# One fused two-block kernel: the coordinate gates and the folding of the wavelet weights put into the first convolution's stage, and a new order of work in the wavelet stage

## The reference, cut to what is touched

```python
# coordinate gate: depends on weights and on positions only, never on x
hdn  = relu(einsum('oi,bihw->bohw', w1, coords) + b1)      # 2 -> 32 channels
gate = sigmoid(einsum('oi,bihw->bohw', w2, hdn) + b2)      # 32 -> 192 channels
# per level l = 0 (64x64) and l = 1 (32x32):
cx = wt_fwd(cur)                        # 2x2 Haar step, 4 bands per channel
t  = dwconv(cx, dw_w[l]); t = einsum('coi,bcihw->bcohw', mix_w[l], t) + mix_b[l]
t  = t * gate[l]
hlow = strip_pool(t, 3); ho = hl*hlow + (1+hh)*(t-hlow)    # 7-wide means
vlow = strip_pool(ho, 2); vo = vl*vlow + (1+vh)*(ho-vlow)
t  = t*beta + vo*gamma
t  = t * sigmoid(einsum('coi,bci->bco', sb_w[l], mean(t)) + sb_b[l]) * wscale[l]
# then both levels back up (iwt), times sigmoid(fuse_gate), plus the 5x5
# depthwise "base" convolution; channel mean/max and row sums for attention
```

## Time and profile before

| what | value |
|---|---|
| median of 3 runs | 2800.9 us (2799.82 to 2801.34) |
| the profiled execution's own time | 2798.28 us |
| its span, first to last instruction | 2796.5 us |
| granted TensorE clock, mean | 0.916 of full |
| PE busy | 2339.4 us (84%) |
| DVE busy | 1596.0 us (57%) |
| ACT busy | 1013.3 us (36%) |
| POOL busy | 536.7 us (19%) |

### The profile page before, as it was taken

How to read it: one execution, slowest core, us unless ns; L and a number is a source line. 1 busy time by engine, 2 the same in 40 slices (tenths; PEclk the granted TensorE clock), 3 DMA queues, 4 the chain that set the end, 5 groups by cost and what they waited for, 6 DMA issues and landing times. The chain is left out here.

```text
span 2796.5 us, 62141 instructions
## 1 busy us (share of the span) xinstructions
PE 2339.4 (84%) x21290; PEld 1273.4 (46%) x21290; DVE 1596.0 (57%) x2838; ACT 1013.3 (36%) x1923; POOL 536.7 (19%) x833
## 2 busy tenths in 40 slices
PE   5767749999969999997399999999994999688887
PEld 2333438777743333331156666666662232233332
DVE  3334411111127777775078888888882445477776
ACT  3344411111118888884100000000000112377776
POOL 7510000000000000003055555665550000000000
PEclk9888869999989999996579999999997899799999
DMA  6987888777737777774655555555543999433332
GB/s 140 249 224 208 212 250 276 267 266 261 270 91 137 147 147 147 147 143 99 133 117 129 123 129 132 130 129 121 130 107 87 229 250 267 120 102 107 103 104 79
DMA packets 550647, 454.97 MB, mean 163 GB/s; under 512 B 335272, under 2 KB 464480, under 8 KB 547136
## 3 DMA queue, kind: packets, MB, share of 16 engines
q1 hardware_dynamic: 417490, 418.23, 57.0%
q10 hardware_dynamic: 129024, 15.75, 4.8%
q0 software_dynamic: 4032, 19.53, 2.9%
HBM read 270.23 MB, written 183.74 MB: 162 GB/s over the span
## 5 line engine op out<-in xcount | busy, mean ns | idle before, releaser
L556 PE MATMUL gate_ps<-gate_data,gate_wt 64*64 64x289 f32 x6144 | 384.3, 408 | 53.2 <-DMA gate_data<-y 39.6
L556 PEld LDWEIGHTS gate_ps<-gate_data,gate_wt 64*64 64x64 f32 x6144 | 311.9, 133 | 125.6 <-issue 60.3
L875 ACT CAST mix_h<-mix_bank 96x512 f16<-96x512 f32 x512 | 267.6, 593 | 7.0 <-PE mix_bank L826 3.2
L596 DVE TENSOR_TENSOR gate_out<-gate_gelu,gate_ps 128x578 f32<-128x578 f32 x96 | 72.6, 757 | 345.0 <-PE gate_ps L556 339.4
L1137 POOL MEMSET cg_image<- 48x7680 f32 x1 | 6.5, 6491 | 1131.7 <-POOLq L58 1131.7
L286 DVE COPY exp_out<-exp_y 128x384 f32<-128x384 f32 x192 | 102.8, 567 | 154.6 <-PE exp_y L249 153.0
L573 ACT ACTIVATE gate_gelu<-gate_ps 128x578 f32<-128x578 f32 x96 | 62.7, 653 | 351.6 <-PE gate_ps L556 351.6
L2012 PE MATMUL fus_bank<-fus_xt,fus_taps 76*32 76x512 f32 x1344 | 159.5, 626 | 27.2 <-DMA fus_shift<-gate_shift 24.3
L957 DVE TENSOR_SCALAR mix_hb<-mix_h,mix_b1q 96x1024 f16<-96x1024 f16 x256 | 122.7, 479 | 93.6 <-ACT mix_h L875 93.6
L826 PE MATMUL mix_bank<-mix_xq,mix_w1q 112*96 112x512 fp8e5 x512 | 143.5, 382 | 29.1 <-ACT mix_h L875 23.0
L965 DVE CAST mix_hq<-mix_hb 96x2048 fp8e5<-96x2048 f16 x128 | 156.5, 1223 | 19.8 <-DVE mix_hb L957 17.9
(11 more groups left out here) (220 smaller groups left out, 4316.8 us busy)
## 6 DMA issues: line engine op xcount, KB each, us to landing
y<-exp_out SPq DMA_DIRECT2D x64, 816.0 KB, 12.3
gate_data<-y SPq DMA_DIRECT2D x24, 2176.0 KB, 15.2
g<-gate_out SPq DMA_DIRECT2D x48, 578.0 KB, 3.6
mix_sc<-g SPq DMA_DIRECT2D x31, 816.0 KB
gate_wt<-wm SPq DMA_DIRECT2D x96, 256.0 KB, 4.8
wav_strips<-xp SPq DMA_DIRECT2D x96, 204.0 KB, 2.9
wav_halves<-xp SPq DMA_DIRECT2D x48, 340.0 KB, 4.4
wav_conv<-wav_lines ACTq DMA_DIRECT2D x384, 40.0 KB
```

What stands on the lines that cost most here:

```text
L556: mm = pe.matmul(banks(a, v)[64 * g:64 * (g + 1), r], wt[q][64 * r:64 * (r + 1), 2 * a + g, n, :], src, start=n == 0, stop=n == 3)
L875: act.copy(h16[at.pair][:, m, h, :], bank[(2 * m + h) % len(bank)][0:HID, :]).then_inc(h16_ready, 1)
```

## The change

Four things change.

1. The stage `coordinate_gates` is gone. Its gate maps are made at the head of `gated_conv`: ACT and GpSimd load the small inputs, PE does ten 2-row and twenty 32-row matmuls before its first convolution matmul, ACT does 3 relus and 10 sigmoids of 1024 columns, and SP stores 20 blocks in runs of 4 KB. SP no longer waits for `cleared` before its first loads, and `data_in` is split by v.
2. The weight folding runs on GpSimd inside `gated_conv` (`wavelet_weights`), behind the gates' stores and the first items. DVE's coefficient tables now stand at the head of the wavelet stage, behind its memsets.
3. In the wavelet's laps PE does `up` for done, after `band_conv_0`, in place of `up` for tail at the end; `low_band` waits for `ct_ready` of two channels back. DVE takes `gate_0` before `add_base`, splits `box_0` around `sums`, and takes `weigh` before `gate_1`.
4. ACT takes over the reflected columns of `init`, the scaled matrices, `logit_w` and `base_w` (from DVE and GpSimd); four of the eight `conv1` loads go to SP; `conv0` and `low_w` become one tile, `front_w`, with one load per half.

```diff
 def gated_conv
             @block.sync
-                sp.wait_ge(cleared, 1)
                 load_weights(0, 0)
                 load_data(0, 0)
+                sp.wait_ge(data_in[0][0], 16)
...
             @block.tensor
+                pe.wait_ge(coords_in, 16 * 10)
+                for n, groups in enumerate((4, 4, 2)):
+                    for g in range(groups):
+                        x = pe.matmul(hidden_banks[n][HD * g:HD * (g + 1), :], cg_w1[HD * g:HD * g + 2, n // 2, :],
+                                      xy[HD * g:HD * g + 2, n, :], start=True, stop=True)
+                pe.wait_ge(maps_in, 16 * 9)
+                pe.wait_ge(relued, 3)
+                for j, (lvl, m, g) in enumerate(JOBS):        # 10 jobs
+                    if j > 1:
+                        pe.wait_ge(gate_ready, j - 1)
+                    for r in range(2):
+                        x = pe.matmul(ps[1][j % 2][0:HID, NT * r:NT * (r + 1)],
+                                      cg_w2[HD * g1:HD * (g1 + 1), lvl, HID * m:HID * (m + 1)],
+                                      hid[2 if lvl else r][HD * g1:HD * (g1 + 1), :], start=True, stop=True)
+                pe.wait_ge(gate_ready, len(JOBS))
...
+            @block.gpsimd
+                pool.wait_ge(gates_out, 16 * 2 * len(JOBS))
+                pool.wait_ge(out_ready, 2 + 8)
+                wavelet_weights(nc, pool, t, tab, k, stage)
 def wavelet
             @block.tensor
                 def low_band(i, u):
+                    if second(i):
+                        pe.wait_ge(ct_ready, 2 * i + u - 1)
                 def step(front, tail, done):
                         band_conv_0(*front)
+                    if done is not None:
+                        up(*done)
                     if tail is not None:
                         mix(*tail)
...
                         base_conv(*front)
-                    if tail is not None:
-                        up(*tail)
             @block.scalar
+                    for lvl, box, scaled in ((0, box0, scaled0), (1, box1, scaled1)):
+                        for m in range(2):
+                            x = act.activation(scaled[u][:, m, :], box[:, :], ACT.Copy, scale=table(coefs[lvl], n)[:, 2 + m:3 + m])
...
             @block.vector
                 def step(front, tail, done):
+                        gate_0(*front)
                         add_base(*done)
-                        gate_0(*front)
-                        box_0(*front)
+                        box_0(*front, 0)
                         sums(*tail)
-                        gate_1(*front)
+                        box_0(*front, 1)
                         weigh(*tail)
+                        gate_1(*front)
                         collect(*done)
```

More of the change, by code:

```diff
@@ L514, in _ @@
                 load_data(0, 1)
+                for j, (lvl, m, g) in enumerate(JOBS):
+                    sp.wait_ge(gate_ready, j + 1)
+                    for o2 in range(2):
+                        if lvl == 0:
+                            at = S1 * g + P8 * (2 * m + o2)
+                            to = t["gate0"][:, at:at + P8].rearrange("c i r x -> c (i r x)")
+                        else:
+                            at = S1 * (2 * m + o2)
+                            to = t["gate1"][:, at:at + S1].rearrange("c i x -> c (i x)")
+                        sp.dma_start(to, stage[C * o2:C * (o2 + 1), j]).then_inc(gates_out, 16)
                 with sp.Fori(0, GROUPS // 2 - 1) as i:
@@ L1558, in _ @@
                 load_act_tables(nc, act, SIGMOID)
+                act.activation(everywhere_all(everywhere, "fuse_gate"), everywhere_all(everywhere, "fuse_gate"),
+                               ACT.Sigmoid).then_inc(fuse_ready, 1)
                 def load_conv1(i, u):
                     c = 2 * i + u
[L1562 removed]
+                    if second(i):
+                        act.wait_ge(conv1_done, c - 1)
+                    for g in range(2, 4):
                         for r in range(2):
[L1564 to L1569 removed]
+                            act.dma_start(*conv1_rows(c, u, g, r)).then_inc(in_conv1[u], 16)
@@ L1598, in step @@
                         low_out(*front)
+                    if done is not None:
+                        reflect_init(*done)
                     if tail is not None:
                         squash(*tail)
+                    if continues(front):
+                        load_conv1(front[0] + 1, front[1])
                     if front is not None:
-                        if continues(front):
-                            act.wait_ge(conv1_done, 2 * front[0] + front[1] + 1)
-                            load_conv1(front[0] + 1, front[1])
                         base_out(*front)
+                    if front is not None and (front[1] == 0 or continues(front)):
+                        matrices_of(front[0] + front[1], 1 - front[1])
                 run(act, step)
@@ new lines, in both @@
+                def both(make):
+                    for l in range(2):
+                        x = make(l, lambda name: levs[l][:, :, columns_of(LEVEL_COLS, name)].rearrange("p c o -> p (c o)"))
+                    chain.link(x)
+                both(lambda l, col: dve.tensor_scalar(hh[:, l], col("hori_high"), 1.0, None, ALU.add))
+                both(lambda l, col: dve.tensor_scalar(vh[:, l], col("vert_high"), 1.0, None, ALU.add))
+                both(lambda l, col: dve.tensor_tensor(hdif[:, l], col("hori_low"), hh[:, l], ALU.subtract))
@@ new lines, in _, with boxes @@
+                for e in range(2):
+                    for a in range(2):
+                        x = dve.tensor_tensor(
+                            up_cols1[:, :, 2 * e:2 * e + 2, 2 * a:2 * a + 2], low_cols,
+                            ih[1][:, :, 2 * e + a].unsqueeze(2).unsqueeze(3).broadcast_to([128, C, 2, 2]), ALU.mult)
+                x.then_inc(tables_ready, 1)
+                def boxes(n, tt, s2, s4, uu, s, edges, at, ready, part):
+                    if part == 0:
+                        dve.wait_ge(edges, n + 1)
+                        dve.tensor_tensor(s2[:, :, :], tt[:, :, 0:s + 5], tt[:, :, 1:s + 6], ALU.add).then_inc(at, 1)
+                        dve.wait_ge(at, 3 * n + 1)
+                        dve.tensor_tensor(s4[:, :, :], s2[:, :, 0:s + 3], s2[:, :, 2:s + 5], ALU.add).then_inc(at, 1)
+                    else:
+                        dve.wait_ge(at, 3 * n + 2)
+                        dve.tensor_tensor(uu[:, :, :], s4[:, :, 0:s], s2[:, :, 4:s + 4], ALU.add).then_inc(at, 1)
+                        dve.wait_ge(at, 3 * n + 3)
+                        dve.tensor_tensor(uu[:, :, :], uu[:, :, :], tt[:, :, 6:s + 6], ALU.add).then_inc(ready, 1)
@@ L1729, in gate_1 @@
                     reflect(t1[u], S1, edged1)
-                    boxes(n, t1[u], s2_1, s4_1, u1[u], S1, edged1, box1_step, u1_ready)
+                    for part in range(2):
+                        boxes(n, t1[u], s2_1, s4_1, u1[u], S1, edged1, box1_step, u1_ready, part)
                 def weigh(i, u):
@@ L1759, in step @@
                 def step(front, tail, done):
+                    if front is not None:
+                        gate_0(*front)
                     if done is not None:
@@ L2260, in build @@
     expand(nc, t)
-    gated_conv(nc, t)
-    token_mix(nc, t, "mix0", t["g"], t["woutT"], None, t["x"], t["w1T_0"], t["b1_0"], t["w2T_0"],
-              t["b2_0"], t["x2"], t["xp"])
     with ExitStack() as st:
@@ L2268, in build @@
         tab = {"levels": [table(f"levels{l}", [128, C, NLEVEL]) for l in range(2)],
-               "coefs": [table(f"coefs{l}", [128, C, 4]) for l in range(2)],
-               "everywhere": table("everywhere", [128, C, NALL]),
-               "up0": table("up0", [128, C, 4]), "up1": table("up1", [128, C, 4, 4])}
-        coordinate_gates(nc, t, tab)
+               "everywhere": table("everywhere", [128, C, NALL])}
+        gated_conv(nc, t, tab)
+        token_mix(nc, t, "mix0", t["g"], t["woutT"], None, t["x"], t["w1T_0"], t["b1_0"], t["w2T_0"],
+                  t["b2_0"], t["x2"], t["xp"])
         wavelet(nc, t, tab)
```

467 lines of the change are left out of this document (204 added, 263 removed).

## The result

| | before | after |
|---|---|---|
| median of 4 runs | 2800.4 us | 2698.2 us (2695.5 to 2706.5) |
| ratio, 95% interval | | 0.9626, 0.959 to 0.9661 |
| profiled execution, span | 2798.3, 2796.5 | 2706.5, 2704.7 |

The account below looks back on a forecast made before the run. It took PE to bound gated_conv, and PE and DVE waiting in turn to bound the wavelet's lap. 2798.3 - 92.3 + 31 + 0 + 1 - 38 = 2700, so 2702 us as median; range of 8 in 10: 2677 to 2734.

Parts of the forecast that it names:

- The stage that goes, -92.3: Between expand and gated_conv's neighbours: removing coordinate_gates, with nothing in its place before the wavelet, saves 92.3 us.
- The gates at the head, +31: Head of gated_conv: the gate work makes PE's first convolution matmul come near 436 in place of 405.3, +31 us.
- Twenty take 34.9 us at that level: Head of gated_conv: the twenty gate matmuls, at 1.745 us each and a clock of 0.50, take 34.9 us.
- the gates run at full clock: Rival, 13%: the gate matmuls at gated_conv's head run at full clock, saving 17 us, 2685 in all.
- The folding on GpSimd, 0: Inside gated_conv: the weight folding fits on idle GpSimd and costs 0, one long clear 4 us at most.
- The wavelet's head, +1: Start of the wavelet: DVE's tables hide behind first loads and convolution, low_out may come later; +1 us, ends -3 and +6.
- The lap, -38: Wavelet laps: PE's waits for sums and weigh go, a lap takes 13.42 in place of 14.30 us, -38 us.
- The clock's dips I leave as they are: Wavelet laps: time lost to clock falls stays unchanged; a rival at 8% had half of 20 us going, 2690.
- The laps keep most of their time: Rival, 20%: GpSimd and DVE hold each other up in wavelet laps; 13.9 us laps give 2724, 14.3 give 2740.
- Slower than before: Rival, 2%: low_band waits for weigh in every wavelet lap; slower only from a lap of 15.7 us.

Follow-up runs that it names:

- e8: Changed kernel with gated_conv's small loads first, gate jobs on four bank pairs, and ACT's conv1 loads ahead of tables and first matrices in the wavelet: 2673.8 us, ratio 0.9544.
- e1: Changed kernel with GpSimd's large folding stores (8.3 MB) sent only after the last product of the convolution: 2726.7 us, ratio 0.9741.
- e9: e8 with the whole folding moved from gated_conv to GpSimd in mix0, its stores in 35 pieces: 2730.3 us, ratio 0.9774.
- e5: Changed kernel with VectorE's lap order of before, PE keeping its new order: 2918 us, ratio 1.0436.
- e11: Changed kernel with both PE's and VectorE's lap orders as before, ACT keeping the work it took over: 2827 us, ratio 1.0104.
- e3: Changed kernel with the folding's stores cut by channels into 35 pieces, one after each pair of products: 2689.4 us, ratio 0.9613.

## Why the prediction came out, step by step

- **The stage that goes, -92.3**: right.
- **The gates at the head, +31**: measured +28.7, by errors that offset each other. "Twenty take 34.9 us at that level" priced matmuls on different row groups as if they stood in line; the ten jobs took 23.4 us, as banks and sigmoids paced them. That is 11.5 us less. Counted from the stage's first instruction, the first small matmul came at 17.3 us, where I had the last load at 13.5, and with 2-row matmuls and relus the jobs began at 23.5 in place of 15.5: 8 us more. A table load for GELU (1.28 us, behind the last sigmoid) was missing. The same head took 48.7 to 54.5 us in nine other runs, so the term is +28 to +34 and its closeness is partly luck. The clock stayed at 0.50, so "the gates run at full clock" fell. The Trainium skill (TensorEngine Tiling (Array Packing), Key Properties) says that tiles of the array run matmuls in parallel; this case's trace agrees (0.65 us each in e8 against 1.745).
- **The folding on GpSimd, 0**: this step failed, by +40. I counted GpSimd's instructions and VectorE's lock, and not the 10.8 MB that its stores put on engines at 0.74 of their time. e1 shows 33 us of it, e9 all but 2. The row was there to read. The Trainium skill (DMA: Bandwidth & Descriptors, Issuing engines are not separate DMA queues) says that transfers started from any engine end on the same sixteen; e1 agrees (without GpSimd's large stores VectorE's wait for SP's stores of g fell from 71.1 to 30.4 us).
- **The wavelet's head, +1**: +3.5, inside its bounds. I had 3 us for low_out behind the loads and the first matrices, and the same back from the second lap. In e8, where low_out no longer stands behind them, the second low_band comes 24.4 us behind the stage's start in place of 29.0, so the term was worth 4.6.
- **The lap, -38**: the waits went as followed (sums and weigh in time, VectorE idle in front of sums), but the step was mis-sized: -83. Of it 20 are falls of the clock that went with the waits (46 laps at 14.74 against 14.30), 40 the 0.88 of rows 5 over 46 laps, and 22 the 0.48 by which a lap without waits is shorter than the busy time of rows 5 (12.94 against 13.42). "The clock's dips I leave as they are" was wrong. I had it as a rival at 8% and half the size. "The laps keep most of their time" fell: the holds by GpSimd are there, 0.7 us in the lap shown, and VectorE's slack takes them.
- **Slower than before** fell for this kernel. That one late wait a lap can cross the line is real, as e5 shows, but it is the wait for sums in front of logit, not the one for weigh in front of low_band that I had named.

## What to carry to other kernels

An engine that is idle is not free capacity if what it does ends in transfers: add up their time on the shared transfer engines, by the share in the trace and not by GB/s, before pricing work "hidden" beside a stage. One engine's order is judged only beside the other's: PE's new order gained 0.43 us a lap beside VectorE's new one, and lost 1.7 beside the old one (17.44 against 15.72). Look at laps with and without a fall of the clock apart: in e5 the order itself cost 1.69 us a lap, and the falls of the clock made it 4.50. To find the floor of a lap, take the distances between the starts of rows that follow each other without a wait, not their lengths.

## What the runs showed of the hardware that was not expected

- A wait of PE costs more than itself. Over the laps the mean granted clock was 1.00 without waits, 0.97 with 0.53 and 0.35 us a lap (before), 0.91 with one of about 1.05 on average (e11) and 0.82 with one of 1.41 (e5). In e5 base_conv took up to 5.35 us in place of 2.82, and 2.8 of the 4.5 us that a lap lost came with the clock.
- Stores from 48 partitions on GpSimd's queue took 6.6 us of all sixteen engines for a MB when cut into pieces (e3) and 4.6 whole (changed kernel), SP's transfers beside them 2.7. Whether queue, partitions or the shifted addresses make the difference was not tried.
- Four buffers turned 71 us of VectorE's waits for g into one wait of PE for weights, with 7 us gained. Here the buffers moved a shortage of transfer time and did not end it.
